# Gram products of a DLRM tower: one 26 by 26 product per sample in a 32-column strip of the PE array, in place of one product per four samples

## The reference, cut to what matters

```
e = jnp.stack([tbl_0[ids[:, 0]], ..., tbl_26[ids[:, 26]]], axis=1)      # (2048, 27, 128), fp32
interactions = jnp.einsum('bfd,bgd->bfg', e, e).reshape(B, F * F)
z = jnp.concatenate([bottom_mlp_out, interactions[:, TRIL_IDX]], axis=1)
h = jnp.concatenate([z, bottom_mlp_out], axis=1)                        # (2048, 607)
h = jnp.maximum(h @ W_top1 + b_top1, 0.0)                               # 512
h = jnp.maximum(h @ W_top2 + b_top2, 0.0)                               # 256
y = h @ W_top3
```

## Time and profile before

| | |
|---|---|
| median of 3 runs | 419.7 us (418.31 to 420.82) |
| the profiled execution | 419.41 us, its span 417.6 us |
| PE (TensorE matmul) busy | 378.1 us, 91% of the span |
| PEld (weight loads) busy | 363.0 us, 87% |
| POOL (GpSimd) busy | 288.1 us, 69% |
| DVE (VectorE) busy | 203.1 us, 49% |
| ACT (ScalarE) busy | 157.4 us, 38% |
| mean granted TensorE clock | 0.988 of full speed |
| chain of waits, by engine | PE 71%, DMA 12%, POOL 8%, issue 4%, ACT 3% |
| chain of waits, by line | one-hot L742 26%, grams L775 18% and L771 3%, layer 1 L783 9%, gathers 8% and their landing 7%, layer 2 L811 7% |

### The profile page before, as it was taken

The page is one execution under the profiler, slowest core; times in us unless marked ns, Lnnn a source line. Parts: engine busy times, 40 slices in busy tenths (PEclk is TensorE's granted clock), DMA queues, the critical chain, the costliest instruction groups (busy, mean ns, idle before and its releaser), DMA issues.

```text
span 417.6 us, 8875 instructions
## 1 busy us (share of the span) xinstructions
PE 378.1 (91%) x3158; PEld 363.0 (87%) x3158; DVE 203.1 (49%) x493; ACT 157.4 (38%) x305; POOL 288.1 (69%) x279
## 2 busy tenths in 40 slices
PE   0457899959999989999899999999999999999987
PEld 0446789959999988999799998999999998999976
DVE  4587337924259124753349234744268235824140
ACT  2243342434332543235332453235423542335343
POOL 6777778777777778777777777777777777750000
PEclk9998999988999999999999999999999999999999
DMA  7999943557245661544324771645334652540000
GB/s 116 243 231 225 261 116 103 95 95 125 67 107 90 107 138 43 124 96 98 122 80 113 99 142 44 135 88 113 104 102 97 103 132 51 138 84 2 2 2 0
DMA packets 49790, 44.19 MB, mean 106 GB/s; under 512 B 30309, under 2 KB 42093, under 8 KB 49767
## 3 DMA queue, kind: packets, MB, share of 16 engines
q1 hardware_dynamic: 39440, 24.26, 30.9%
q0 software_dynamic: 8704, 17.84, 16.5%
q10 hardware_dynamic: 1623, 1.79, 1.6%
HBM read 39.01 MB, written 4.85 MB: 105 GB/s over the span
## 4 chain that ended last, share of the span: by engine, by line
PE 71%; DMA 12%; POOL 8%; issue 4%; ACT 3%; DVE 1%; SPq 1%; ACTq 0%; POOLq 0%
PE ps_build L742 26%; PE ps_gram L775 18%; PE ps_dense L783 8%; POOL rows L400 8%; DMA rows<-tbl_dram,idx 7%; PE ps_dense L811 6%; DMA raw<-tbl_dram 5%; PE ps_gram L771 3%; PE ps_build L754 2%; PE ps_dense L819 2%; PE ps_gram L754 2%; PE ps_gram L783 1%; ACT embT L561 1%; PE ps_build L811 1%; DVE table L415 1%
## 5 line engine op out<-in xcount | busy, mean ns | idle before, releaser
L400 POOL DMA_INDIRECT rows<-tbl_dram,idx x272 | 287.4, 1056 | 84.4 <-issue 77.4
L742 PE MATMUL ps_build<-hot,table 125*128 125x256 f32 x1280 | 164.2, 288 | 26.0 <-DVE table L415 18.4
L742 PEld LDWEIGHTS ps_build<-hot,table 125*128 125x128 f32 x1280 | 158.2, 194 | 26.8 <-issue 21.4
L440 DVE TENSOR_SCALAR hot<-id_raw 125x512 fp32r<-125x512 f32 x320 | 120.4, 435 | 5.5 <-PE ps_build L742 4.1
L775 PEld LDWEIGHTS ps_gram<-embT 128*107 128x107 f32 x896 | 89.8, 177 | 6.5 <-issue 3.0
L454 DVE COPY gram<-ps_gram 107x416 f32<-107x416 f32 x56 | 32.9, 588 | 125.0 <-PE ps_gram L775 120.6
L775 PE MATMUL ps_gram<-embT 128*107 128x104 f32 x896 | 92.4, 262 | 1.4 <-ACT embT L561 0.8
L554 ACT COPY embT<-ps_build 128x512 f32<-128x512 f32 x40 | 32.1, 804 | 108.6 <-PE ps_build L742 102.3
L573 ACT COPY gram<-ps_gram 107x416 f32<-107x416 f32 x56 | 28.4, 506 | 52.5 <-PE ps_gram L775 49.9
L783 PE MATMUL ps_dense<-pairT,w1p 120*128 120x256 f32 (+1 forms) x252 | 34.8, 283 | 0.0
L783 PEld LDWEIGHTS ps_dense<-pairT,w1p 120*128 120x128 f32 (+1 forms) x252 | 32.2, 191 | 0.0
(11 more groups left out here) (60 smaller groups left out, 169.4 us busy)
## 6 DMA issues: line engine op xcount, KB each, us to landing
id_raw<-ids_onehot_dram SPq DMA_DIRECT2D x40, 256.0 KB, 5.9
gram_dram<-gram SPq DMA_DIRECT2D x56, 84.5 KB
raw<-tbl_dram SPq DMA_DIRECT2D x10, 448.0 KB
rows<-tbl_dram,idx POOLq DMA_INDIRECT x272
bot<-bottom_dram SPq DMA_DIRECT2D x8, 128.0 KB, 6.5
w1p_raw<-w_pairs_dram ACTq DMA_DIRECT2D x1, 720.0 KB
raw<-tbl_dram SPq DMA_DIRECT2D x10, 52.0 KB
w2s<-w_dram ACTq DMA_DIRECT2D x1, 512.0 KB
```

What stands on the lines that cost most here:

```text
L400: nc.gpsimd.indirect_dma_start(rows[:, t, s * D:(s + 1) * D], None, tables[f], bass.IndirectOffsetOnAxis(idx[:, 2 * i + t, f:f + 1], 0)).t ...
L440: last = nc.vector.tensor_scalar(hot[0:VP, a % HOT_SLOTS, v, 0:w, :], shifted, float(v0 + v), None, ALU.is_equal)
L742: last = nc.tensor.matmul(bank[:, q * HALF:(q + 1) * HALF], table[0:VP, units[n][q], bits, row:row + D], hot[0:VP, a % HOT_SLOTS, v, q, :] ...
```

## The change

`pair_products` now makes one product per sample: 26 stationary columns, 26 moving columns, 128 partitions deep, with `tile_position=(0, 32 k)` for sample k of a group of four. Sample k's result goes to PSUM partitions 32 k to 32 k + 25. A half so has 256 gram products, 512 pairs. Sixteen groups fill one bank (16 times 26 = 416 columns), and a tile fills two banks; tile 0 uses the banks of `ps_gram[0]`, tile 1 those of `ps_gram[1]`, and TensorE waits for no eviction within a half. VectorE empties the first bank of a tile with one copy of 122 by 416 and ScalarE the second, in all eight halves alike. `embT` has 27 columns a sample in half 7 too, and the memset of its padding is gone.

What moves with it: layers 2 and 3 stand behind all grams of tile 1 and no longer between its steps. VectorE's and ScalarE's work on the pairs of the half before (`pairs_low`, `pairs_high`) stands ahead of their copy of tile 0. The one-hot parts of the next half are made three after tile 0's copy and two after tile 1's. `gram` has a place of its own for each tile, so the copy of tile 1 waits no more for the write of tile 0.

```diff
-    GB = 8
-    GU = TILE // GROUP // GB
-    GRAMS = 2 * GU
-    GC = GROUP * PG
+    GB = JT // 2
...
-        gram = in_arena("gram", [GM, GROUP, PG, JT], fp32, 0)
+        gram = in_arena("gram", [GR, 2, PG, JT], fp32, 0)
...
-        emb_flat = sb("embT", [128, HALF * PAD], fp32)
...
+        embT = sb("embT", [128, HALF, FEATURES], fp32)
...
+        def gram_piece(i, t, b):
+
+            src = gram_banks[2 * t + b][0:GR, 0:GB * PG].rearrange("p (g n) -> p n g", n=PG)
+            if is_half(i, LAST):
+                return gram_end[:, :, t * JT + b * GB:t * JT + (b + 1) * GB], src
+            return gram[:, t, :, b * GB:(b + 1) * GB], src
...
-            def pair_products(i, t, u):
-
-                v = t * GU + u
-                if u == 0:
-                    pe.wait_ge(emb_done, BUILDS * i + nth("tile", t, TQ - 1) + 1)
+            def pair_products(i, t):
+                pe.wait_ge(emb_done, BUILDS * i + nth("tile", t, TQ - 1) + 1)
                 for b in range(2):
-                    if v >= 2 and (b == 0 or is_half(i, LAST)):
-                        pe.wait_ge(gram_dve, GRAMS * i + v - 1)
-                    if v >= 2 and (b == 1 or is_half(i, LAST)):
-                        pe.wait_ge(gram_act, GRAMS * i + v - 1)
-                    for g in range(GB // 2):
...
+                    for g in range(GB):
+                        for k in range(GROUP):
+                            x = embT[:, t * TILE + (b * GB + g) * GROUP + k, :]
+                            last = nc.tensor.matmul(gram_banks[2 * t + b][PAD * k:PAD * k + PG, g * PG:(g + 1) * PG],
+                                                    x[:, 0:PG], x[:, 1:FEATURES], start=True, stop=True,
+                                                    tile_position=(0, PAD * k))
                     last.then_inc(grammed[b], 1)
...
             def second_tile(i, dense=None):
-                for u in range(GU):
-                    pair_products(i, 1, u)
-                    if dense is not None and u < M2:
-                        layer2(dense, u)
-                    if dense is not None and u == M2:
-                        layer3(dense)
+                pair_products(i, 1)
+                if dense is not None:
+                    for m in range(M2):
+                        layer2(dense, m)
+                    layer3(dense)
```

More of the change, by code:

```diff
@@ L486, in half, with grams @@
                     split_weights()
-                for u in range(GU):
[L488 to L498, removed]
+                for c in range(3):
+                    pairs_low(i - 1, c)
+                grams(i, more)
+            def grams(i, more=True):
+                for t in range(2):
+                    empty_gram(i, t)
+                    for a in ((0, 1, 2), (3, 4))[t] if more else ():
+                        make_hot(i + 1, a)
             dve.wait_ge(consts_made, 1)
@@ L506, in _ @@
                     split_table(q)
-            for n in range(GRAMS):
-                empty_gram(FIRST, n // GU, n % GU)
-                if n >= GRAMS - HOT_SLOTS:
-                    make_hot(1, n - GRAMS + HOT_SLOTS)
+            grams(FIRST)
             half(1)
@@ L553, in emb_hot @@
                 f = NG + units[p][0]
-                nc.scalar.copy(emb(i)[:, :, f:f + n], src).then_inc(emb_done, 1)
+                nc.scalar.copy(embT[:, :, f:f + n], src).then_inc(emb_done, 1)
             def emb_tile(i, t, u):
@@ L626, in first_tile @@
             def first_tile(i, dense=None):
-                for u in range(GU):
-                    empty_gram(i, 0, u)
-                    if dense is not None and u < 3:
-                        pairs_high(dense, u)
+                if dense is not None:
+                    for c in range(3):
+                        pairs_high(dense, c)
+                empty_gram(i, 0)
             def second_rows(i, dense=None):
@@ L639, in second_tile @@
             def second_tile(i, dense=None):
-                for u in range(GU):
-                    empty_gram(i, 1, u)
-                    if dense is not None and u < M2:
-                        layer2(dense, u)
-                    if dense is not None and u == M2:
-                        layer3(dense)
+                empty_gram(i, 1)
+                if dense is not None:
+                    for m in range(M2):
+                        layer2(dense, m)
+                    layer3(dense)
             def half(i, dense):
@@ L852, in first_tile @@
             def first_tile(i):
-                for u in range(GU):
-                    pair_products(i, 0, u)
+                pair_products(i, 0)
             def second_rows(i, dense=None):
```

72 lines of the change are left out of this document (16 added, 56 removed).

## The result

The changed kernel takes **455.6 us** (median of four executions, 449.8 to 457.4) where the kernel before takes 419.0 beside it: a ratio of 1.079, 95% interval 1.066 to 1.092. The profiled execution took 454.5 us, its span 452.6 us against 417.6.

What follows compares the result with a forecast made beforehand. Gathers bound the kernel up to 200.27 us, TensorE's own work after. Half 7's point forward 4 us, last tile's grams -2.7, relayout -0.8, layer 3 +0.35: -7.2 on 419.4 us gives 412 us, range 403 to 450.

Steps and rivals of the forecast that it cites:

- Grams after: Gram products of the changed kernel: 512 pairs a half at 16 ns, a tile's gram 4.1 us where it was 6.2.
- The sum: Whole kernel: gains limited by gathers, then last grams, relayout and layer 3, together -7.2 us on 419.4, giving 412 us.
- four rivals: One line 434 us, chance 0.25; floor near break-even 420, 0.13; no overlap 550, 0.20; gathers leave no room 416, in first case.
- The pace: Gram pairs in four strips: 16 ns a pair taken, range 15 to 20, loads for different strips overlapping.
- The gain of an own half: Halves 4 to 6, bound by TensorE: 3.5 us each, from 2 x 2.1 - 0.4 - 0.35.
- the 0.35 taken: Layer 3, no longer covered by a gram step: 0.35 us a half lost, within 0 to 0.6.
- the 0.4 taken for four seams: Switches between whole-array and strip matmuls, four a half: 0.1 us each, at most 0.17, at least nothing.
- The gathers: Row gathers limit the gain: half 6 forward by 1.4 us, half 7 by 4; TensorE waits for rows in halves 4 to 6.
- the first case: Likeliest case, loads overlapping in different strips: 412 us, own range 404 to 416, chance 0.42.
- A clock that falls because short products use the array less: TensorE's granted clock, counted in the rival of strips without overlap: 550 us, anything from 32 ns a pair up; chance 0.20.
- Evictions and the relayout: PSUM copies become 16 and 16 of about the same length, nothing gained in the loop; the relayout begins without its wait.
- That term of -0.8: Relayout at the program's end: -0.8 us, as the last copy now lies under layers 2 and 3 of half 6.

Runs made afterwards that it cites:

- e9: Changed kernel with the first instruction of TensorE's loop body laid on the start of a 16 KB instruction block: 408.9 us, ratio 0.973 to the kernel before.
- e10: As e9, but with the loop's head at slot 208 of the block instead of 0: median 426.8 us, four executions of 410.1 to 446.3 us.
- e2: Changed kernel leaving out every second group's gram products, 128 a half instead of 256: 394.3 us, ratio 0.936 to the kernel before.
- e4: Kernel before changed to two samples a product in two strips of 64 columns, 128 products a half: 401.4 us, ratio 0.957.
- e13: e4 with TensorE's loop begun at half 1 and its head on an instruction block's start: 401.6 us, ratio 0.959 to the kernel before.
- e7: Changed kernel without the row gathers of halves 1 to 7: median 444.7 us, three executions at 444.7 to 446.7, one at 419.0.
- e16: Changed kernel without the reads of the pairs back from DRAM in halves 2 to 7: 414.8 us (409.7 to 426.1), ratio 0.980 to the kernel before.
- e5: Changed kernel with a branch-prefetch hint for the closing branch at the head of TensorE's loop body: 410.4 us, ratio 0.976 to the kernel before.
- e6: Kernel before with three one-column filler products ahead of each gram product, no strips: 741.4 us, ratio 1.747.

## Why the prediction was wrong

**The failed step** is in "Grams after" and "The sum": I costed 384 more pairs a half by TensorE's array alone and gave no time to bringing their instructions. All four rivals were about the array's pace or the gathers; none asked where instructions come from. The page of before had the row (13 packets), and the chain's two short "issue" waits at one-hot products showed that TensorE can wait for them, but I read neither. It cost 62.5 us of waits (47.9 + 19.5 - 4.9), and the lower clock behind them came on top. Against e9, which has the same products and a span 46.0 us shorter, 37.3 us are waits for instructions (67.4 less 30.1) and 9.1 us are longer busy time of TensorE (352.3 for 343.2, at a mean clock of 0.910 for 0.954).

The Trainium skill has the rule that I should have weighed (Runtime: NRT & Kernel Launch, Instruction fetch mechanics): instructions come in blocks of 16 KiB, 256 each, into a buffer of 128 KiB for TensorE; crossing a block is "mostly hidden", and a taken branch to a block outside a window of two stalls. The packets of 16 KB agree. "Mostly hidden" does not, where a block lasts 2 us and comes in 3.5 to 9. Nor does the window of two blocks: e9's body is six blocks long and its loop turns without a wait. By the page's 2048 instructions for TensorE, an estimate would have the doubled body, some 1,600 with its waits and branches, just fit; e10 shows that it then hangs on where it begins.

**The pace** was right: 16 ns taken, 15.6 ns measured (3.99 us for 256), and a tile at 4.0 to 4.1 us. Its working was not: within a run pairs mostly start 6 to 12 ns apart, and five or six gaps of 0.2 to 0.3 us in each tile, with nothing fetched, make up the rest. What those gaps are stays open, so the agreement of 16 with 15.6 is in part luck.

**The gain of an own half** was right too: 3.5 us forecast, 45.85 to 42.15 us in the mean of e9's halves 3 to 6. In its half 4 the two grams take 8.07 us where they took 12.45. From its chain, around layers 1, 2 and 3:
```profile
243.43 1.64 PE ps_dense L734 x12
...
254.44 3.67 PE ps_dense L762 x16
258.11 0.52 PE ps_dense L770 x2
258.63 0.04 issue
258.68 0.59 PE ps_dense L770 x2
```
and the same work in half 5 before:
```profile
288.88 1.46 PE ps_dense L783 x12
...
297.12 1.75 PE ps_dense L811 x8
...
303.62 0.95 PE ps_dense L819 x4
```
Layer 3 without its cover costs 0.20 us (1.15 for 0.95), for the 0.35 taken. The first layer-1 step behind the strips costs 0.18 and layer 2 behind them 0.17 (3.67 for twice 1.75); against the 0.4 taken for four seams that is about right, though what the two ways into the strips cost can't be told from the grams' own 8.07. The one-hot products behind layer 3 cost 0.23 more (7.93 for 7.70), where before a gram step stood behind it.

**The gathers** were right as a limit and wrong in their times. I took the gather of group 3 of tile 1 in half 6 to begin at 325.39 us however early TensorE came, so that half 6 could come forward by 1.4 us only. In e9 it begins 11 us earlier, and its transposes 6.8 us earlier:
```profile
314.41 1.09 POOL L381 DMA_INDIRECT rows<-tbl_dram,idx  x1 [0.30 <-issue]
...
331.06 0.60 PE L717 MATMUL ps_build<-ident,rows 128*128 128x128 f32 x4
```
A gather's mean went from 1.056 us to 1.011, for a reason that stays open, so a half's 34 take 44.3 us instead of 45.9. That is still slower than halves of 42 us: the time from this gather's start to its transposes shrinks by 2 us a half in e9, 22.9, 20.7, 18.8, 16.7 and 14.8 us in halves 3 to 7. It lasts to the end because it began so large, behind TensorE's waits of 9.5 and 6.2 us for instructions in halves 1 and 2. Where there are no such waits, the forecast waits for rows are there: halves 3 to 6 take 44.3 us in the mean in e2, 45.0 in e4 and 44.6 in e13, about what their gathers take. So behind the fetch the next limit is the one that I named. That e9's 408.9 us lie in the first case's 404 to 416 is therefore luck: half 3 begins 8.3 us later than before, where I had no loss, and halves 3 to 6 gain 16.7 us together. A slip besides: in half 7 the best landing (6.45 us) leaves 6.8 us, not 5.7.

**The clock.** "A clock that falls because short products use the array less" was a rival of 550 us. The clock did fall, but after waits for instructions, and not in halves without them.

**Evictions and the relayout.** The copies fell to 14 of 588 and 14 of 506 ns in halves 0 to 6, and TensorE waited for none of them, as said. The relayout's wait did not go: it is 0.78 us, for the copy of y, where 0.82 was. That term of -0.8 was wrong: layers 2 and 3 of half 6 now stand right ahead of the relayout, and its first bank waits for their y.

What stays open: why the unaligned loop is fetched in every second turn rather than in each, why the times of one kernel differ as if by whole refetched turns (e7, e10, e16), and whether it is the hint in e5 or the shift that it brings.

## What to carry to other kernels

Splitting a product into small ones multiplies instructions, and here somewhere between 518 and 774 pairs a loop body, or in code that runs once, that has a price of its own. So look at the packets of the instruction queue, at "issue" in the chain at places where operands were ready, and at whether equal turns of a loop take equal times. Ask then for fewer instructions at the same saving (two samples a product in strips of 64 columns took 401.4 us with no care for the loop; one sample a product took 401.7 with the loop lengthened, aligned and the products spread), for a loop that stays resident (its head aligned), and for no burst of transfers beside a burst of instructions. A term that is right where the code is resident says nothing of the turns where it isn't.

## What the runs showed of the hardware that I had not expected

- A TensorE loop body of 518 pairs stayed resident unaided, one of 774 pairs did so with its head on a block's start or with a branch hint in it (408.9 and 410.4 us), and without either alternated: 42 and 63 to 66 us for the same work.
- Instruction packets wait behind another queue's traffic: TensorE's wait was 8.6 us with the pair reads beside them, 1.0 to 1.4 us without, and unchanged (8.2 to 9.3 us) without the gathers.
- Strip products of 26 columns run at 15.6 ns a pair and of 52 columns in two strips at 26 ns, where 104 columns on the whole array take 98 ns.
- One-column products between those of 104 columns let the granted clock fall to 0.50 with TensorE busy throughout (15.00 of 15 us, e6); 512 strip products a half leave it at 1.00.
